# Moving half of GpSimd's scaled copies to ScalarE in a Mamba scan kernel

## The reference, cut to what matters

```
def step(h, inp):
    xt, dtt, Bt, Ct = inp
    dA = jnp.exp(dtt[:, :, None] * A)
    h = dA * h + (dtt * xt)[:, :, None] * Bt[:, None, :]
    y = jnp.einsum('ben,bn->be', h, Ct)
    return (h, y)
...
y = ys.transpose(1, 0, 2) + xc * Dp
y = y * _silu(z)
return y @ W_out.T
```

## Time and profile before

| what | us |
|---|---|
| median of 3 runs | 12582.62 (12567.47 to 12611.38) |
| the profiled execution | 12573.23 |
| its span | 12571.4 |
| busy in the span: VectorE, GpSimd, ScalarE, TensorE | 11844.0, 11416.9, 10843.1, 10178.1 |

### The profile page before, as it was taken

One profiled execution on the slowest core, in us unless ns is written; L12 is line 12 of the kernel. 1 busy time (PEld: TensorE's weight loads), 2 busy tenths in 40 slices (PEclk: granted clock), 3 DMA queues, 4 the chain that ended last, 5 costly groups with the idle time before them and its releaser, 6 DMA issues.

```text
span 12571.4 us, 179496 instructions
## 1 busy us (share of the span) xinstructions
PE 10178.1 (81%) x51484; PEld 5823.6 (46%) x51484; DVE 11844.0 (94%) x7037; ACT 10843.1 (86%) x23461; POOL 11416.9 (91%) x5971
## 2 busy tenths in 40 slices
PE   7668878888787887878888787887878878788887
PEld 3334545444454444544445444454544445444445
DVE  7999999999999999999999999999999999999991
ACT  7888988899898888988898888898888989888882
POOL 6999999999999999999999999999999999999992
PEclk8779989899898999999999898998989999998898
DMA  3223334333343333333333333333433333343332
GB/s 100 91 93 110 125 106 129 115 118 124 107 130 113 123 124 111 122 113 127 124 110 118 112 129 116 116 129 102 134 114 122 119 115 123 112 129 124 105 110 96
DMA packets 610170, 1457.99 MB, mean 116 GB/s; under 512 B 68944, under 2 KB 110064, under 8 KB 604704
## 3 DMA queue, kind: packets, MB, share of 16 engines
q1 hardware_dynamic: 609056, 1445.13, 35.5%
HBM read 1354.04 MB, written 90.83 MB: 115 GB/s over the span
## 4 chain that ended last, share of the span: by engine, by line
issue 27%; PE 21%; ACT 18%; POOL 16%; DVE 15%; DMA 1%; DVEq 0%; POOLq 0%; SPq 0%; ACTq 0%
POOL state L1419 12%; DVE state L1387 11%; ACT state L1184 6%; ACT v_sb L1197 6%; PE driven L974 5%; PE q_ps L929 4%; DVE driven L1376 3%; PE y_ps L996 3%; PE q_ps L916 2%; PE p_ps L834 2%; PE b_ps L964 1%; PE p_ps L845 1%; POOL v_sb L1499 1%; ACT L1184 1%; PE p_ps L861 1%
## 5 line engine op out<-in xcount | busy, mean ns | idle before, releaser
L1419 POOL TENSOR_TENSOR state<-state,c_rep 128x1024 f32<-128x1024 f32 x4096 | 9660.4, 2389 | 780.0 <-DVE state L1387 773.3
L1387 DVE TENSOR_TENSOR_SCAN state<-state,driven 128x1024 f32<-128x1024 f32 x4096 | 9095.8, 2270 | 274.5 <-PE driven L974 262.6
L1184 ACT ACTIVATE state<-ud_rep,cols_sb 128x512 f32<-128x512 f32 x8192 | 5212.4, 710 | 3.4 <-PE y_ps L996 1.2
L1197 ACT ACTIVATE v_sb<-u_t,b_t 128x128 f32<-128x128 f32 x12288 | 4062.9, 506 | 944.5 <-PE driven L974 940.4
L974 PE MATMUL driven<-consts_sb,v_sb 128*128 128x128 f32 x16384 | 2635.4, 314 | 1314.8 <-DVE state L1387 1293.3
L974 PEld LDWEIGHTS driven<-consts_sb,v_sb 128*128 128x128 f32 x16384 | 2134.7, 161 | 2491.0 <-DVE state L1387 1799.7
L996 PE MATMUL y_ps<-state,consts_sb 128*32 128x512 f32 x16384 | 2391.9, 660 | 545.0 <-POOL state L1419 543.2
L1376 DVE TENSOR_TENSOR driven<-ud_rep,b_ps 128x1024 f32<-128x1024 f32 x2048 | 2390.3, 1213 | 0.9 <-issue 0.9
L929 PE MATMUL q_ps<-hid,wq_sb 128*128 128x256 f32 x7936 | 2028.3, 400 | 143.2 <-ACT hid L1162 78.7
L929 PEld LDWEIGHTS q_ps<-hid,wq_sb 128*128 128x128 f32 x7936 | 1463.3, 194 | 989.3 <-issue 803.5
L1499 POOL TENSOR_TENSOR v_sb<-u_t,b_t 128x512 f32<-128x512 f32 x1024 | 1069.3, 1044 | 23.4 <-issue 23.4
(11 more groups left out here) (170 smaller groups left out, 5523.1 us busy)
## 6 DMA issues: line engine op xcount, KB each, us to landing
c_rep<-bc_rows SPq DMA_DIRECT2D x2048, 256.0 KB, 3.0
ud_rep<-ud_rows SPq DMA_DIRECT2D x512, 512.0 KB, 4.0
wq_sb<-in_h SPq DMA_DIRECT2D x512, 512.0 KB, 3.9
wq_sb<-in_f SPq DMA_DIRECT2D x128, 512.0 KB, 4.1
wp_sb<-in_win SPq DMA_DIRECT2D x64, 512.0 KB, 4.1
ud_rows<-u_pad SPq DMA_DIRECT2D x128, 256.0 KB, 3.4
ud_rows<-dt_sb SPq DMA_DIRECT2D x128, 256.0 KB, 3.5
u_nat<-ud_rows SPq DMA_DIRECT2D x128, 256.0 KB, 3.0
```

The costliest lines, as they stand in the source:

```text
L1184: ins = act.activation(state[:, unit % STATE_RING, j, :], ud_rep[:, nth % 2, j, 1, :], ACT.Exp, scale=a_neg[:, d, c, j, g:g + 1])
L1197: ins = act.activation(v_sb[:, unit // 2 % V_RING, tt, :, :, n].rearrange("p j e -> p (j e)"), u_t[:, nth % 2, tt, :], ACT.Identity, scale ...
L1387: dve.tensor_tensor_scan(flat, flat, driven[:, q % DRIVE_RING].rearrange("p j t -> p (j t)"), 0.0, ALU.mult, ALU.add).then_inc(scanned, 1)
L1419: pool.tensor_tensor(part, part, c_rep[:, unit % ROW_RING, :].unsqueeze(1).to_broadcast([P, 2, T]), ALU.mult).then_inc(was_read, 1)
```

## The change

GpSimd's copy (tt = 3) is made only for every second odd unit: 1, 5, 9, ... (`POOLED_UNITS`). For units 3, 7, 11, ... ScalarE makes tt = 2 and 3 in its odd turn, 8 ACTIVATEs instead of 4. The waits on `v_pooled` count accordingly.

```
+POOLED_UNITS = PE_UNITS[::2]
...
-                    pe.wait_ge(v_pooled, v_count(at, unit))
+                    if unit in POOLED_UNITS:
+                        pe.wait_ge(v_pooled, of_body(at, len(POOLED_UNITS), POOLED_UNITS.index(unit) + 1))
...
-                            act.wait_ge(v_pooled, of_body(at, len(PE_UNITS), 0 if d else len(PE_UNITS) // 2))
+                            act.wait_ge(v_pooled, of_body(at, len(POOLED_UNITS), 0 if d else len(POOLED_UNITS) // 2))
...
-                        act.wait_ge(v_pooled, of_body(at, len(PE_UNITS), NG // 2 * (nth - 1)))
+                        act.wait_ge(v_pooled, of_body(at, len(POOLED_UNITS), NG // 4 * (nth - 1)))
...
-                for tt in (2,) if part else (0, 1):
+                own = TT - 1 if unit % UNITS in POOLED_UNITS else TT
+                for tt in range(2, own) if part else (0, 1):
...
-                    if unit % 2 == 0 and (at.kind in SCAN_PARTS if ahead < UNITS else at.has("next")):
+                    if ahead % UNITS in POOLED_UNITS and (at.kind in SCAN_PARTS if ahead < UNITS else at.has("next")):
                         make_v(at, ahead)
```

## The result

| | before | after |
|---|---|---|
| median of 16 runs each, side by side | 12584.2 us | 12625.83 us (12617.12 to 12646.61) |
| ratio, 95% interval | | 1.0033 [1.0025, 1.004] |
| the profiled execution | 12573.23 | 12630.38 |
| its span | 12571.4 | 12628.6 |
| a middle batch, mean of fourteen | 765.23 | 769.18 |

The change costs 41.6 us by the medians; 12632 was predicted. The two profiled executions are 57 us apart: fourteen middle batches of 3.95 us each give 55, and the rest lies ahead of and behind them.

The account below looks back on a forecast made before the run. VectorE was taken as the bound, only its idle time changing: losses 7.1 less gains 3.8 make 3.3 us a batch, times 15 is 50 us, 12623 from the profiled run, 12632 us as median; range 12560 to 12720.

Parts of the forecast that it names:

- Losses at units 29, 39, 97 and 108: B rows, dt projection, a later ScalarE copy, softplus: ScalarE late, VectorE loses 1.4, 1.2, 1.1 and 1.1 us a batch.
- Units 57 and 125: TensorE stands still for a GELU, one added ScalarE set in each run: losses of 1.1 and 1.2 us a batch.
- Unit 110: Softplus logarithm, then VectorE's add: later start hidden inside GpSimd's second product, loss 0; without that cover 1.2 us.
- Units 16, 21 and 25, 76: VectorE waits caused by GpSimd, which has fewer copies ahead: gains of 0.9, 0.8 and 1.5 us a batch.
- Unit 71: VectorE idle 0.60 us where GpSimd is late: gain 0.6 us a batch.
- Units 79 and 91: GpSimd late, but TensorE also waits for weights or a ScalarE copy: gain taken as 0, up to 1.0 us each.
- ScalarE's idle time for v_sb: Sign of being right: ScalarE's waits for a v_sb slot, 940 us, fall by 500 to 600 us in all.
- VectorE's busy time: Sign of being right: it stays within 20 us, with the blocked add of unit 110 getting shorter.
- Rival 4: GpSimd's freed time only becomes waiting for the scans, only losses remain: 107 us, 12690 us; chance 0.08.
- Rival 1: ScalarE's reserve hides the added copies and GpSimd's relief wins: -3.8 us a batch, 12526 us; chance 0.1.
- rival 3: ScalarE becomes a second bound, twelve to fifteen places lose 1.2 us: 12 us a batch, 12765 us; chance 0.1.
- Rival 2: Losses and gains cancel through further covers or units 79 and 91: 1.3 us a batch, 20 us, 12603 us; chance 0.32.

Follow-up runs that it names:

- e6: Kernel before the change, with only units 31, 55 and 111 moved from GpSimd's copy to ScalarE; 12613.29 us.
- e10: Changed kernel plus 9 and 11 unused TensorE matmuls ahead of the GELU waits of units 57 and 125; 12585.97 us, ratio 1.0000.
- e9: e5 plus 9 unused TensorE matmuls ahead of each of the two GELU waits; 12432.16 us, ratio 0.9880.
- e2: Kernel before, GpSimd omitting its copies for units 3, 7, 11, ..., ScalarE not making them (TensorE transposes block 2 again); 12500.39 us, ratio 0.9938.
- e4: Kernel before, with ScalarE taking GpSimd's copy only for units 11, 15, 19, 23, 47, 71 and 75; 12547.18 us, ratio 0.9963.
- e1: Kernel before, GpSimd keeping its copies, ScalarE also making the change's extra copies into a tile nobody reads; 12699.37 us, ratio 1.0099.
- e3: The change with the other odd units: ScalarE takes over 1, 5, 9, ..., GpSimd keeps 3, 7, 11, ...; 12636.49 us, ratio 1.0049.
- e5: e4, with GpSimd also making block 2 for units 31, 55, 99, 107, 111 and 123 in place of ScalarE; 12452.95 us, ratio 0.9894.
- e8: Changed kernel plus 14 and 18 unused TensorE matmuls ahead of the GELU waits of units 57 and 125; 12631.79 us, ratio 1.0037.
- e7: e5, with units 79 and 91 also moved to ScalarE and block 2 of units 39 and 87 to GpSimd; 12469.89 us, ratio 0.9903.

## Why the prediction was right, and where its terms were off

The time, the sign and the mechanism were right: VectorE's idle time is what moved (5.6 us a batch, against 1.7 of busy time), ScalarE's added copies stretch it at six named places, and GpSimd's relief fills it at others.

- **Losses at units 29, 39, 97 and 108** were priced at 1.4, 1.2, 1.1 and 1.1 and measured 1.2, 1.3, 1.0 and 1.0. One set behind ScalarE's last idle moment is the whole price; e6 shows the same for unit 29 with one set in that run instead of every second one.
- **Units 57 and 125** are the mis-sized terms: 1.1 and 1.2 predicted, 1.7 and 1.85 measured. I priced TensorE's standstill and left the speed of what follows it unchanged. The earlier trace rows had the hint: eight rows took 2.55 us at the one place and 3.60 at the other. With TensorE kept busy both excesses are gone (e10, e9). But e2 and e4 have part of this loss without one more copy on ScalarE ahead of it, so it does not belong to the added copies alone; what sets the moment at which the clock falls stays open.
- **Unit 110** was priced at nothing because of GpSimd's product, and so it was: idle time up 1.17, busy time down 1.18.
- **Units 16, 21 and 25, 76** gained 1.0, 1.1 and 1.8, each a little more than the 0.9, 0.8 and 1.5 predicted. I had subtracted at unit 76 what unit 71 was to use up, and unit 71 used nothing. That units 21 and 25 are GpSimd's gain is not clean, since in e1 unit 21 lost its idle time as well.
- **Unit 71** is the step that failed: 0.6 gain predicted, 0.3 loss measured. GpSimd did come in time, but TensorE had another wait ahead of it in the queue, for ScalarE. The prediction names such a case at unit 91 and did not look for it here.
- **Unit 48** gained 0.75 and unit 13 0.26, which the list of places did not have; units 0 and 45 lost 0.6.
- **Units 79 and 91** came out at nothing on the mean, but not by standing still: before, unit 91 had 1.34 to 1.37 us in every middle batch, after 1.05 to 1.07 or 2.01 to 2.03, and unit 79 between 0.48 and 2.99. What picks the one or the other in a batch stays open.
- **ScalarE's idle time for v_sb** was to fall by 500 to 600 us and fell by 281. I had read the 940 us as ScalarE's whole idle time, but they are only its waits for v_sb; all its idle time was 1728 us (12571.4 less 10843.1) and fell by 505, so the rest came from its other waits. It changed nothing in the sum.
- **VectorE's busy time** was to stay within 20 us and fell by 28 (11844.0 to 11816.0), of which unit 110 is about 17. The scans took 2.27 us and not the 2.2 that the prediction writes; no term hangs on it.

Losses were too small by 2.1 us a batch and gains by 1.2, 0.5 us of busy time went that no step had, and 0.2 of idle time came in units that the table leaves out: the net of 3.3 stands against 3.95. A part of the agreement is thus luck, errors that pull against each other. Against the profiled execution, 12623 stands against 12630.4. The rise of 50 us that was predicted lies between the 41.6 of the medians and the 57 of the two profiled executions, so the time alone would not tell 3.3 from 3.95. Rival 4 (freed time of GpSimd is only waiting) is refuted by e2, where relief alone takes off 81 us. Rival 1 (ScalarE's reserve hides it) and rival 3 (a second bound) are refuted by e1: the losses alone are 118 us, neither nothing nor the 240 of sixteen us a batch. Rival 2 (20 us) was nearest; its two sources did not show, since units 79 and 91 gave nothing and the busy time changed by over 0.1 us at no unit but 110.

Open is why unit 115 has 1.5 to 2.0 us of idle time in some batches and none in the others, in one batch before, five in e1, six in e2 and eleven in e4, with TensorE's clock at 1.00; and why e3 gains nothing at unit 48. Both lie some units behind the nearest change of load. Each kernel has one profile, so idle times of a unit are those of one execution.

## What to carry to other kernels

When work moves between two engines that both have idle time, do not compare the idle time: list the places where the bounding engine waits, name for each who is last in the chain, and find in that engine's rows the last idle moment ahead of it. Only what lies behind that moment counts, and at the places read here it counted nearly whole (1.0 to 1.3 us for a set of 1.2); so moves of such copies can cost (e3, 1.0049) or, in both directions to whoever has slack, gain (e5, 0.9894). Behind a standstill of TensorE, read the length of its next rows too, and before a wait is removed ask which operation of the other engine the freed instruction will now meet.

## What the runs showed of the hardware that was not expected

- Behind a standstill of TensorE of 3.30 us the eight rows that follow took 2.55 us at a clock of 0.77 (before), behind one of 4.29 us 3.77 at 0.50 (after). The length does not decide: behind 3.30 us (e4), 3.41 us (e5) and 3.47 us (e6) they also took 3.78, 3.77 and 3.78. Unused matmuls in the standstill kept it at 1.00, window of e9 over its unused matmuls and over the two rows behind them:

```profile
4957.40:4961.20 3.80, 3.80 (x22) 3.36 (x19) 3.80 (x4) 3.77 (x4) 3.80 (x3) 1.00 0.38 138
4961.40:4963.00 1.60, 1.60 (x9) 1.42 (x8) 1.60 (x2) 1.59 (x3) 0.97 (x2) 1.00 0.39 49
4963.10:4964.00 0.90, 0.90 (x9) 0.78 (x7) 0.90 (x1) 0.90 (x3) 0.90 (x1) 1.00 1.10 385
```

- Such filler has a price of its own: a float32 matmul of 256 columns is two rows, 0.45 us together at the upper clock (6.31 us for 14, 4.15 for 9). Nine and eleven at the two GELUs gave 40 us over the change (e10), fourteen and eighteen gave nothing (e8).
- VectorE's operation over 128x2048 ended 2.15 us behind GpSimd's product wherever the two met, whether VectorE had come 2.2 us (before), 1.05 us (after) or 4.2 us (e7) ahead of the product's end. All 374 operations of this size that took over 2.62 us, in the twelve traces, ended 2.14 to 2.16 us behind one. In e7 VectorE waited through two products in a row, though it had started during the first. GpSimd can be the one that waits: at unit 40 of before VectorE's first operation took 2.60 us and GpSimd's product beside it 4.41 instead of 2.4, and VectorE's add behind that 4.34 instead of 2.29. This last wait stands in every middle batch of the kernel before, and neither the prediction nor the change touches it.
